# Graph attention block on one core: another order of work ahead of the first weight product

## The chip, the cores and the metric

The kernel runs on one core of one Trainium2 chip, as one program launch. The metric is the device time of that core in microseconds (us). TensorE, VectorE, ScalarE, GpSimd and SyncE (the queue SP, which only starts transfers here) each have their own instruction stream and meet at semaphores.

## The reference

With x of 384 rows by 1024 features, h = relu(layernorm(x)), and then a graph attention of 16 heads whose projections each consist of two matrices in a row:

```python
h = jnp.maximum(_layernorm(x, axis=-1), 0.0)
q = x @ wq.T + bq;   k = x @ wk.T + bk;   v = x @ wv.T + bv          # x is h here
q2 = (q @ wiq.T + biq)...; k2 = (k @ wik.T + bik)...; v2 = (v @ wiv.T + biv)...   # 16 heads of 64
mask = _build_mask(edge_index, edge_type, edge_type_weights, x.dtype)  # 384x384, from 6528 edges
scores = einsum('hnd,hmd->hnm', q2, k2) * scale + mask[None]
out = einsum('hnm,hmd->hnd', softmax(scores), v2)
return x + out @ wo.T + bo
```

(The lines are run together here.) Everything is float32. The part that the change touches is the layer norm of h and the first two of the eight column tiles of v = h @ wv.T + bv.

## The kernel before, in words

**Split numbers.** TensorE multiplies in a reduced form of float32 (fp32r). So each operand is kept as a high part (the value rounded by a copy, `..._hi`) and a low part (value minus high part, `..._lo`), and each product of two 128-wide blocks is three matmuls: high by high, low weight by high activation, high weight by low activation (`products`, L849, L850, L851). A weight slab is 128x1024 numbers; a stage of 1024 output columns has eight. A slab is fetched by SP into one of three places of `raw` (L305), ScalarE makes its high part (`split_hi`, L456), VectorE or GpSimd its low part (`split_lo`, L712 and L374), and TensorE then does one tile with it: 8 blocks k of the contraction times three matmuls of 384 columns. A place of `raw` comes free for the next transfer when the low part is made.

**The beginning.** The rows of x come as three tiles t of 128 rows (`x_sb`). For each, VectorE takes the statistics (L679, L683) and the variance plus epsilon (L685), GpSimd raises it to the power -1/2 (`rstd`, L367, after `memset`s and an `iota`), and for tiles 0 and 1 ScalarE makes h in one operation (L476). Tile 2 is the last and is done in another way, in halves of 512 columns: VectorE subtracts the mean and takes the maximum with 0 (L689, both halves while GpSimd works on the power), then ScalarE multiplies the first half by `rstd` in two pieces of 256 columns (L482, semaphore `h_ok`), and VectorE the second half (L693, `h_last_ok`). TensorE turns h in blocks of 128x128 (`turn_h`, L894) so that features lie on partitions: block k of all three tiles goes to one PSUM bank, `h_bank[k]`. When the block of tile 2 is there (`h_turned`), ScalarE copies the bank to `a_hi[k]` (L486, `h_hi`), and VectorE makes `a_lo[k]` from bank and high part (L725, `h_lo`). Blocks are turned as their scalings come: 0 to 6 of tiles 0 and 1 at once, with dummy matmuls (`warm`, L890, counts in `WARM`) between, block 7 of all tiles only inside the first tile.

**The first slab.** Its high part is made in halves: the first by ScalarE (L467, `half_hi`), the second by VectorE after the scaling (L695, `early_hi`). GpSimd makes both low parts (L384; `half_lo`, then `slab_lo`), and then, whole, that of slab 1 (L374).

**The first tile** (`first_tile`, L922, L923, L929) does for each k high by high, low weight, low activation. Its first matmul waits for `half_lo` and `h_hi`. The three late turns of tile 2 stand behind its second matmul. Tile 1 and all later ones are done by `tile` (L849 to L851), which waits for the whole low part of its slab. ScalarE's order between the copies to `a_hi` is written out: five of them, then the high part of slab 1, then three more, then the high part of slab 2.

Of the kernel before, what the change touches and what calls it, by code (L numbers as in the profile page):

```python
# [20 lines left out]
P = 128  # L21
N = 384
# [30 lines left out]
WARM = [18, 4, 3]  # L53
# [17 lines left out]
def gat_kernel(nc, slabs, x, edge_cols, edge_rows, edge_weights, biases, bo, out):  # L71
    with ExitStack() as ctx:
# [89 lines left out]
        h_bank = [bank[4], bank[7], bank[3], bank[5], bank[0], bank[1], bank[2], bank[4]]  # L162
# [31 lines left out]
        half_hi, half_lo, early_hi = sem("half_hi"), sem("half_lo"), sem("early_hi")  # L194
# [9 lines left out]
        y_ok, out_done, out_ok, stored = sem("y_ok"), sem("out_done"), sem("out_ok"), sem("stored")  # L204

# [137 lines left out]
        def _(pool):  # L343
# [107 lines left out]
        def _(act):  # L451
# [16 lines left out]

            for t in range(NT):
                act.dma_start(x_sb[:, t, HALF:F], x[t * P:(t + 1) * P, HALF:F]).then_inc(x_in[t][1], 16)  # L470
            for t in range(NT):
# [127 lines left out]
        def _(dve):  # L599
# [123 lines left out]
            for k in range(KT):  # L723
                dve.wait_ge(h_hi, k + 1)
                nc.vector.tensor_tensor(a_lo[:, k, :], h_bank[k][:, 0:N], a_hi[:, k, :].bitcast(F32),  # L725
                                        ALU.subtract).then_inc(h_lo, 1)
            edge_sign()
# [118 lines left out]
        def _(pe):  # L846
# [10 lines left out]
            def tile(t, a_h, a_l, ks=range(KT)):  # L857

                hi, lo = split_slab(slab_of(t))
# [5 lines left out]
                for k in ks:  # L865
                    c = slice(k * P, (k + 1) * P)
                    mm = products(psum[:, 0:N], (hi[:, c], lo[:, c]), (a_h[:, k, :], a_l[:, k, :]), k == 0,
# [24 lines left out]
            def turn_h(k, t):  # L892

                mm = nc.tensor.transpose(h_bank[k][:, t * P:(t + 1) * P], x_sb[:, t, k * P:(k + 1) * P], ident[:])  # L894
# [7 lines left out]
            for t in range(NT - 1):  # L902
                pe.wait_ge(h_ok, t + 1)
                for k in range(KT - 1):
                    turn_h(k, t)
                warm(WARM[t + 1])
            for b in range(2):
                pe.wait_ge(h_ok, NT + b)
                for k in range(2 * b, 2 * b + 2):
                    turn_h(k, NT - 1)  # L910

            def first_tile():

                hi, lo = split_place(0)
                psum = tile_place(0)[3]
                pe.wait_ge(half_lo, 1)
                for k in range(KT):
                    c = slice(k * P, (k + 1) * P)
# [208 lines left out]
```

## Time and profile before

| what | before |
|---|---|
| median of 3 runs | 295.54 us (295.51 to 296.37) |
| the profiled execution | 295.47 us |
| its span | 293.7 us |
| outside the span | 1.8 us |
| TensorE busy | 287.4 us (98%) |
| VectorE, ScalarE, GpSimd busy | 176.7, 153.5, 150.7 us |
| granted TensorE clock, mean | 0.998 |

The span runs from the first to the last instruction. A start in a timeline row is us from the span's start; a second number is how long the row's work took. Instructions of one engine are pipelined: the next may start shortly before the one ahead is shown as ended.

### The profile page before, as it was taken

To read this page: it belongs to the slowest core of one execution; us is meant where nothing else is said; L and a number is where in the kernel's file an instruction comes from. 1 tells how busy PE (TensorE), PEld (TensorE's weight loads), DVE (VectorE), ACT (ScalarE), POOL (GpSimd) and SP (SyncE) were. 2 spreads that over 40 slices of the span, in tenths; PEclk is the share of its full clock that TensorE was granted. 3 is DMA by queue.
4 is the path that set the end of the run, shared out by engine and by line. 5 is a ranking of instruction groups with operands and counts; after the bars stand their busy time and mean duration, and the time that the engine had idled before them with its cause. 6 is when DMAs were issued, how large, how long until landed. Compare 5 with 4: busy or idle time off the path is not lost.

```text
span 293.7 us, 4994 instructions
## 1 busy us (share of the span) xinstructions
PE 287.4 (98%) x1813; PEld 266.4 (91%) x1813; DVE 176.7 (60%) x475; ACT 153.5 (52%) x288; POOL 150.7 (51%) x153
## 2 busy tenths in 40 slices
PE   6899999999999999999999999999999999999996
PEld 3699998888899999999999999999999997888885
DVE  4999778786544534454467766665747475835241
ACT  2876443152523443244324685969687879874100
POOL 6552455543464455545300797758393939874000
PEclk9999999999999999999999999999999999999999
DMA  7978955749733443334654043140403132400032
GB/s 257 332 230 264 315 191 180 232 153 301 270 105 117 139 143 136 91 134 145 182 193 145 0 141 106 46 144 0 145 10 136 41 106 71 144 1 2 0 143 71
DMA packets 15818, 40.84 MB, mean 139 GB/s; under 512 B 3481, under 2 KB 4914, under 8 KB 15794
## 3 DMA queue, kind: packets, MB, share of 16 engines
q1 hardware_dynamic: 13346, 38.53, 39.2%
q0 software_dynamic: 2016, 1.21, 1.8%
q10 hardware_dynamic: 432, 0.79, 0.7%
q8 instruction: 14, 0.23, 0.3%
q14 instruction: 10, 0.08, 0.1%
HBM read 37.71 MB, written 2.81 MB: 138 GB/s over the span
## 4 chain that ended last, share of the span: by engine, by line
PE 95%; DMA 2%; ACT 1%; DVE 0%; SPq 0%; issue 0%
PE banks L849 27%; PE banks L850 26%; PE banks L851 26%; PE banks L966 5%; PE banks L1009 3%; PE banks L1010 3%; PE banks L981 3%; DMA x_sb<-in_x 2%; PE banks L994 1%; PE banks L894 1%; PE banks L922 1%; PE banks L929 0%; PE banks L923 0%; ACT x_sb L476 0%; SPq L289 0%; DVE stats L679 0%
## 5 line engine op out<-in xcount | busy, mean ns | idle before, releaser
L403 POOL DMA_INDIRECT cells<-value,cell x51 | 54.8, 1074 | 59.2 <-DMA cells<-value,cell 45.9
L456 ACT ACTIVATE w_hi<-raw 128x1024 fp32r<-128x1024 f32 x51 | 53.8, 1055 | 17.5 <-PE banks L851 17.3
L849 PE MATMUL banks<-a_hi,w_hi 128*128 128x384 f32 x184 | 61.5, 334 | 0.0
L850 PE MATMUL banks<-a_hi,w_lo 128*128 128x384 f32 x184 | 61.5, 334 | 0.0
L851 PE MATMUL banks<-a_lo,w_hi 128*128 128x384 f32 x184 | 61.5, 334 | 0.0
L712 DVE TENSOR_TENSOR w_lo<-raw,w_hi 128x1024 fp32r<-128x1024 f32 x36 | 44.0, 1223 | 12.6 <-ACT w_hi L456 12.5
L429 POOL TENSOR_SCALAR prob<-prob,row_inv 128x384 f32<-128x384 f32 x36 | 22.5, 640 | 43.6 <-DVE row_inv L779 43.6
L374 POOL TENSOR_TENSOR w_lo<-raw,w_hi 128x1024 fp32r<-128x1024 f32 x15 | 36.0, 2404 | 0.9 <-ACT w_hi L456 0.9
L849 PEld LDWEIGHTS banks<-a_hi,w_hi 128*128 128x128 f32 x184 | 34.5, 188 | 0.1
L850 PEld LDWEIGHTS banks<-a_hi,w_lo 128*128 128x128 f32 x184 | 34.5, 188 | 0.0
L851 PEld LDWEIGHTS banks<-a_lo,w_hi 128*128 128x128 f32 x184 | 34.5, 188 | 0.0
L783 DVE TENSOR_TENSOR pt_lo<-banks,pt_hi 128x384 fp32r<-128x384 f32 x48 | 23.8, 551 | 13.3 <-ACT pt_hi L548 13.1
L461 ACT ACTIVATE b_hi<-banks,bias 128x384 fp32r<-128x384 f32 x16 | 9.3, 581 | 35.0 <-PE banks L851 35.0
L534 ACT ACTIVATE prob<-prob,neg_max 128x384 f32<-128x384 f32 x36 | 21.8, 606 | 9.2 <-DVE neg_max L769 9.2
L548 ACT ACTIVATE pt_hi<-banks 128x384 fp32r<-128x384 f32 x48 | 20.1, 491 | 5.6 <-PE banks L1010 4.5
L849 PE MATMUL banks<-c_hi,w_hi 128*128 128x384 f32 x64 | 22.2, 346 | 0.0
L700 DVE SCALAR_TENSOR_TENSOR b_lo<-banks,bias,b_hi 128x384 fp32r<-128x384 f32 x16 | 9.9, 617 | 20.1 <-ACT b_hi L461 20.1
L849 PE MATMUL banks<-b_hi,w_hi 128*128 128x384 f32 x64 | 21.9, 343 | 0.0
L851 PE MATMUL banks<-b_lo,w_hi 128*128 128x384 f32 x64 | 21.4, 335 | 0.0
L851 PE MATMUL banks<-c_lo,w_hi 128*128 128x384 f32 x64 | 21.4, 334 | 0.0
L850 PE MATMUL banks<-c_hi,w_lo 128*128 128x384 f32 x64 | 21.4, 334 | 0.0
L850 PE MATMUL banks<-b_hi,w_lo 128*128 128x384 f32 x64 | 21.4, 334 | 0.0
(146 smaller groups left out, 610.1 us busy)
## 6 DMA issues: line engine op xcount, KB each, us to landing
raw<-in_slabs SPq DMA_DIRECT2D x56, 512.0 KB, 3.4
work<-key_rows SPq DMA_DIRECT2D x6, 256.0 KB, 5.3
prob<-key_rows SPq DMA_DIRECT2D x6, 256.0 KB, 3.8
x_sb<-in_x SPq DMA_DIRECT2D x3, 512.0 KB, 6.0
out_y<-x_sb SPq DMA_DIRECT2D x5, 256.0 KB, 2.1
cells<-prob SPq DMA_DIRECT2D x2, 576.0 KB, 7.9
cells<-value,cell POOLq DMA_INDIRECT x51, 2.6
x_sb<-in_x ACTq DMA_DIRECT2D x3, 256.0 KB, 4.3
```

The source lines that it names most:

```text
L374: nc.gpsimd.tensor_tensor(lo, raw[:, s % RAW, :], hi.bitcast(F32), ALU.subtract).then_inc(slab_lo, 1)
L403: nc.gpsimd.indirect_dma_start(out=cells[c][:, :], out_offset=bass.IndirectOffsetOnAxis(ap=cell[:, t:t + 1], axis=0), in_=value[:, t:t + 1 ...
L429: nc.gpsimd.tensor_scalar(probs[j % 2][x][:, n, :], probs[j % 2][x][:, n, :], row_inv[:, j % 2, c:c + 1], 1.0, ALU.mult, ALU.mult).then_in ...
L456: nc.scalar.activation(split_place(s)[0], raw[:, s % RAW, :], ACT.Copy).then_inc(slab_hi, 1)
L534: nc.scalar.activation(probs[j % 2][x][:, n, :], probs[j % 2][x][:, n, :], ACT.Exp, scale=-1.0, bias=neg_max[:, j % 2, c:c + 1], accum_out ...
L548: nc.scalar.activation(pt_as_placed(pt_hi, h, m), pt_place(h, m), ACT.Copy).then_inc(pt_hi_ok, 1)
L712: nc.vector.tensor_tensor(lo, raw[:, s % RAW, :], hi.bitcast(F32), ALU.subtract).then_inc(slab_lo_dve, 1)
L783: nc.vector.tensor_tensor(pt_as_placed(pt_lo, h, m), pt_place(h, m), pt_as_placed(pt_hi, h, m).bitcast(F32), ALU.subtract).then_inc(pt_lo_ ...
L849: nc.tensor.matmul(psum, w[0], a[0], start=first, stop=False)
L850: nc.tensor.matmul(psum, w[1], a[0], start=False, stop=False)
L851: return nc.tensor.matmul(psum, w[0], a[1], start=False, stop=last)
L966: mm = nc.tensor.matmul(score_bank(2 * n + x)[:, 0:N], q[own, turn, m], k[own, turn, :], start=(p == 0), stop=(p == 2))
```

## The change

It touches the beginning alone. In words:

1. VectorE does the second half of tile 2's subtract-and-maximum only when the power is there, instead of beside it, and then the multiply.
2. VectorE, not GpSimd, makes the low part of the first slab's first half, before `a_lo[0]`; the high part of the second half moves behind `a_lo[0]`. GpSimd makes only the second half's low part.
3. ScalarE's scaling of tile 2's first half is in pieces of 128, 128 and 256 columns; the third stands behind `a_hi[0]`.
4. TensorE turns all eight blocks of tiles 0 and 1 at once; block 7 goes to columns 384 to 511 of banks 0, 1 and 2. In the first tile, the first matmul waits only for `half_hi` and `h_hi`; the late turns (4 to 7, then 2 and 3, of tile 2) stand behind this one matmul, and the low weight and low activation matmuls of k = 0 and 1 come after.
5. ScalarE copies blocks 2 and 3 only when seven and eight blocks are turned, and makes the high part of slab 1 behind `a_hi[3]`, not behind `a_hi[4]`.
6. GpSimd makes the low part of slab 1 in two halves, and tile 1 starts on the first.
7. The dummy matmuls are 20, 5, 0 and 1 instead of 18, 4 and 3.

```diff
-WARM = [18, 4, 3]
+WARM = [20, 5, 0, 1]
...
-        h_bank = [bank[4], bank[7], bank[3], bank[5], bank[0], bank[1], bank[2], bank[4]]
+        h_bank = bank[0:6] + bank[7:8]
...
+        def h_turned_at(k, t):
+            return h_bank[k][:, t * P:(t + 1) * P] if k < KT - 1 else bank[t][:, N:N + P]
+        def h_all(k):
+            return h_bank[k][:, 0:N] if k < KT - 1 else banks[:, 0:NT, N:N + P]
...
                 hi, lo = split_place(s)
+                if s == 1:
+                    nc.gpsimd.tensor_tensor(lo[:, 0:HALF], raw[:, s, 0:HALF], hi[:, 0:HALF].bitcast(F32),
+                                            ALU.subtract).then_inc(second_lo, 1)
+                    nc.gpsimd.tensor_tensor(lo[:, HALF:F], raw[:, s, HALF:F], hi[:, HALF:F].bitcast(F32),
+                                            ALU.subtract).then_inc(slab_lo, 1)
+                    return
...
-            for b in range(2):
-                half = slice(b * HALF, (b + 1) * HALF)
-                pool.wait_ge((half_hi, early_hi)[b], 1)
-                nc.gpsimd.tensor_tensor(w_lo[:, 0, half], raw[:, 0, half], w_hi[:, 0, half].bitcast(F32),
-                                        ALU.subtract).then_inc((half_lo, slab_lo)[b], 1)
+            pool.wait_ge(early_hi, 1)
+            nc.gpsimd.tensor_tensor(w_lo[:, 0, HALF:F], raw[:, 0, HALF:F], w_hi[:, 0, HALF:F].bitcast(F32),
+                                    ALU.subtract).then_inc(slab_lo, 1)
...
-                    for part in (slice(0, HALF // 2), slice(HALF // 2, HALF)):
-                        nc.scalar.activation(x_sb[:, t, part], x_sb[:, t, part], ACT.Copy,
-                                             scale=rstd[:, t:t + 1]).then_inc(h_ok, 1)
+                    for part in (slice(0, P), slice(P, 2 * P)):
+                        scale_last(part)
             for k in range(KT):
-                act.wait_ge(h_turned, k + 1)
-                nc.scalar.activation(a_hi[:, k, :], h_bank[k][:, 0:N], ACT.Copy).then_inc(h_hi, 1)
-                if k == KT // 2:
+                if k == KT - 1:
+                    act.wait_ge(h_lo, NT)
+                act.wait_ge(h_turned, min(k + 1, KT) if k < 2 else min(k + 1 + KT // 2, KT))
+                nc.scalar.activation(as_turned(a_hi, k), h_all(k), ACT.Copy).then_inc(h_hi, 1)
+                if k == 0:
+                    scale_last(slice(2 * P, HALF))
+                if k == KT // 2 - 1:
                     split_hi(1)
...
                 h_last = x_sb[:, NT - 1, b * HALF:(b + 1) * HALF]
+                if b == 1:
+                    dve.wait_ge(rstd_ok, NT)
                 nc.vector.tensor_scalar(h_last, h_last, mean_var[:, NT - 1, 0:1], 0.0, ALU.subtract,
                                         ALU.max).then_inc(h_step, 1)
-            dve.wait_ge(rstd_ok, NT)
             dve.wait_ge(h_step, 2)
             nc.vector.tensor_scalar(h_last, h_last, rstd[:, NT - 1:NT], None, ALU.mult).then_inc(h_last_ok, 1)
-            dve.wait_ge(slab_in[0], 16)
-            nc.vector.tensor_copy(w_hi[:, 0, HALF:F], raw[:, 0, HALF:F]).then_inc(early_hi, 1)
+            dve.wait_ge(half_hi, 1)
+            nc.vector.tensor_tensor(w_lo[:, 0, 0:HALF], raw[:, 0, 0:HALF], w_hi[:, 0, 0:HALF].bitcast(F32),
+                                    ALU.subtract).then_inc(half_lo, 1)
...
+                if k == 0:
+                    dve.wait_ge(slab_in[0], 16)
+                    nc.vector.tensor_copy(w_hi[:, 0, HALF:F], raw[:, 0, HALF:F]).then_inc(early_hi, 1)
...
+                pe.wait_ge(half_hi, 1)
+                pe.wait_ge(h_hi, 1)
+                nc.tensor.matmul(psum[:, 0:N], hi[:, 0:P], a_hi[:, 0, :], start=True, stop=False)
+                turn_late()
+                pe.wait_ge(h_ok, NT + 2)
+                for k in range(2, KT // 2):
+                    turn_h(k, NT - 1)
+
                 pe.wait_ge(half_lo, 1)
-                for k in range(KT):
-...
+                first_product(0, lo, a_hi)
+                pe.wait_ge(h_hi, 2)
+                first_product(1, hi, a_hi)
+                first_product(1, lo, a_hi)
+                for k in range(2):
+                    pe.wait_ge(h_lo, k + 1)
+                    first_product(k, hi, a_lo)
+                for k in range(2, KT):
                     if k == KT // 2:
                         wait_lo(pe, 0)
                     pe.wait_ge(h_hi, k + 1)
...
```

TensorE's order at the start of the first tile, before (L890 dummy matmuls, L894 turns, L922, L923 and L929 the three matmuls of a block):

```order
L890 MATMUL banks<-iota,above 128x384 x3
L894 MATMUL banks<-ident,x_sb 128x128 [waits h_ok]
L894 MATMUL banks<-ident,x_sb 128x128
L894 MATMUL banks<-ident,x_sb 128x128 [waits h_ok]
L894 MATMUL banks<-ident,x_sb 128x128
L922 MATMUL banks<-a_hi,w_hi 128x384 [waits h_hi,half_lo]
L923 MATMUL banks<-a_hi,w_lo 128x384
L894 MATMUL banks<-ident,x_sb 128x128 [waits h_last_ok]
L894 MATMUL banks<-ident,x_sb 128x128 x2
L929 MATMUL banks<-a_lo,w_hi 128x384 [waits h_lo]
L894 MATMUL banks<-ident,x_sb 128x128 x3
L922 MATMUL banks<-a_hi,w_hi 128x384 [waits h_hi]
```

The same place of the changed kernel (L927 dummy matmul, L931 turns, L966 the first matmul, L962 the others):

```order
L931 MATMUL banks<-ident,x_sb 128x128 [waits h_ok] x2
L927 MATMUL banks<-iota,above 128x384
L966 MATMUL banks<-a_hi,w_hi 128x384 [waits h_hi,half_hi]
L931 MATMUL banks<-ident,x_sb 128x128 [waits h_last_ok]
L931 MATMUL banks<-ident,x_sb 128x128 x3
L931 MATMUL banks<-ident,x_sb 128x128 [waits h_ok]
L931 MATMUL banks<-ident,x_sb 128x128
L962 MATMUL banks<-a_hi,w_lo 128x384 [waits half_lo]
L962 MATMUL banks<-a_hi,w_hi 128x384 [waits h_hi]
L962 MATMUL banks<-a_hi,w_lo 128x384
L962 MATMUL banks<-a_lo,w_hi 128x384 [waits h_lo] x2
L962 MATMUL banks<-a_hi,w_hi 128x384 [waits h_hi]
```

Six turns, two of which were ahead of the first matmul, now stand in one block behind it, and the wait for the low part of the slab has moved from ahead of the first matmul to behind these turns.

ScalarE's order from the first slab's high part on, before (L467 that high part, L482 scalings, L486 copies to `a_hi`, L456 high parts of slabs 1 and 2):

```order
L467 ACTIVATE w_hi<-raw 128x512 [waits slab_in0]
L482 ACTIVATE x_sb<-x_sb,rstd 128x256 [waits rstd_ok,h_step]
L482 ACTIVATE x_sb<-x_sb,rstd 128x256
L486 ACTIVATE a_hi<-banks 128x384 [waits h_turned] x5
L456 ACTIVATE w_hi<-raw 128x1024 [waits slab_in1]
L486 ACTIVATE a_hi<-banks 128x384 [waits h_turned] x3
L456 ACTIVATE w_hi<-raw 128x1024 [waits slab_in2]
```

And of the changed kernel (L484, L488, L509 and L473 in their places):

```order
L484 ACTIVATE w_hi<-raw 128x512 [waits slab_in0]
L488 ACTIVATE x_sb<-x_sb,rstd 128x128 [waits rstd_ok,h_step]
L488 ACTIVATE x_sb<-x_sb,rstd 128x128
L509 ACTIVATE a_hi<-banks 128x384 [waits h_turned]
L488 ACTIVATE x_sb<-x_sb,rstd 128x256
L509 ACTIVATE a_hi<-banks 128x384 [waits h_turned] x3
L473 ACTIVATE w_hi<-raw 128x1024 [waits slab_in1]
L509 ACTIVATE a_hi<-banks 128x384 [waits h_turned] x3
L509 ACTIVATE a_hi<-banks 128x384 [waits h_turned,h_lo]
L473 ACTIVATE w_hi<-raw 128x1024 [waits slab_in2]
```

A third scaling stands between the first two copies, and the high part of slab 1 has moved up past the copy of block 4.

## Rows read from the trace of the kernel before

**Rows 1.** The page: span, TensorE's busy time, and the chain that ended last
```profile
span 293.7 us, 4994 instructions
PE 287.4 (98%) x1813; PEld 266.4 (91%) x1813; DVE 176.7 (60%) x475; ACT 153.5 (52%) x288; POOL 150.7 (51%) x153
...
PE 95%; DMA 2%; ACT 1%; DVE 0%; SPq 0%; issue 0%
```

**Rows 2.** Chain of waits, 8 to 17.5 us: start us, us, what
```profile
11.46 0.50 ACT a_hi L486
...
12.10 0.41 PE banks L922
```

**Rows 3.** Timeline, TensorE: start us, us, line, operation, tiles, shape, count
```profile
12.10 0.41 PE L922 MATMUL banks<-a_hi,w_hi 128*128 128x384 f32 x1 [0.22 <-ACT a_hi L486]
12.35 0.34 PE L923 MATMUL banks<-a_hi,w_lo 128*128 128x384 f32 x1
12.52 0.49 PE L894 MATMUL banks<-ident,x_sb 128*128 128x128 f32 x3
...
13.94 0.34 PE L922 MATMUL banks<-a_hi,w_hi 128*128 128x384 f32 x1
...
16.89 0.34 PE L929 MATMUL banks<-a_lo,w_hi 128*128 128x384 f32 x1
17.07 0.35 PE L849 MATMUL banks<-a_hi,w_hi 128*128 128x384 f32 x1
```

**Rows 4.** Timeline, ScalarE, 9 to 16 us
```profile
10.48 0.91 ACT L482 ACTIVATE x_sb<-x_sb,rstd 128x256 f32<-128x256 f32 x2 [0.16 <-POOL rstd L367]
...
11.46 2.02 ACT L486 ACTIVATE a_hi<-banks 128x384 fp32r<-128x384 f32 x5
...
13.33 1.10 ACT L456 ACTIVATE w_hi<-raw 128x1024 fp32r<-128x1024 f32 x1
...
14.28 1.30 ACT L486 ACTIVATE a_hi<-banks 128x384 fp32r<-128x384 f32 x3
```

**Rows 5.** Timeline, GpSimd, 5.5 to 17 us
```profile
5.78 0.57 POOL L367 TENSOR_TENSOR rstd<-var_eps,minus_half 128x1 f32<-128x1 f32 x1 [1.22 <-DVE var_eps L685]
...
9.63 0.75 POOL L367 TENSOR_TENSOR rstd<-var_eps,minus_half 128x1 f32<-128x1 f32 x1 [1.41 <-DVE var_eps L685]
10.39 1.28 POOL L384 TENSOR_TENSOR w_lo<-raw,w_hi 128x512 fp32r<-128x512 f32 x1
...
12.37 1.28 POOL L384 TENSOR_TENSOR w_lo<-raw,w_hi 128x512 fp32r<-128x512 f32 x1 [0.70 <-DVE w_hi L695]
...
14.50 2.41 POOL L374 TENSOR_TENSOR w_lo<-raw,w_hi 128x1024 fp32r<-128x1024 f32 x1 [0.85 <-ACT w_hi L456]
```

**Rows 6.** Timeline, VectorE, 9 to 19 us
```profile
9.47 0.87 DVE L689 TENSOR_SCALAR x_sb<-x_sb,mean_var 128x512 f32<-128x512 f32 x2
...
10.46 1.50 DVE L693 TENSOR_SCALAR x_sb<-x_sb,rstd 128x512 f32<-128x512 f32 x1
11.87 0.41 DVE L695 CAST w_hi<-raw 128x512 fp32r<-128x512 f32 x1
...
12.21 2.40 DVE L725 TENSOR_TENSOR a_lo<-banks,a_hi 128x384 fp32r<-128x384 f32 x5
...
17.20 1.21 DVE L712 TENSOR_TENSOR w_lo<-raw,w_hi 128x1024 fp32r<-128x1024 f32 x1
```

**Rows 7.** Groups by form, 9 to 17.3 us: count, busy us, mean ns of one
```profile
L725 DVE TENSOR_TENSOR a_lo<-banks,a_hi 128x384 fp32r<-128x384 f32 x8 | 3.9, 546 | 0.2 <-ACT a_hi L486 0.2
...
L482 ACT ACTIVATE x_sb<-x_sb,rstd 128x256 f32<-128x256 f32 x2 | 0.9, 501 | 0.2 <-POOL rstd L367 0.2
L689 DVE TENSOR_SCALAR x_sb<-x_sb,mean_var 128x512 f32<-128x512 f32 x2 | 0.9, 480 | 0.0
```

**Rows 8.** Groups by form, TensorE: dummy matmuls of 2.4 to 5.7, then of 7.4 to 9.5 us
```profile
L890 PE MATMUL banks<-iota,above 128*128 128x384 f16 x11 | 3.7, 520 | 2.5 <-POOL above L357 2.5
...
L890 PE MATMUL banks<-iota,above 128*128 128x384 f16 x4 | 0.8, 326 | 0.0
```

More of the change, by code:

```diff
@@ L193, in gat_kernel @@
         h_turned, h_hi, h_lo = sem("h_turned"), sem("h_hi"), sem("h_lo")
-        half_hi, half_lo, early_hi = sem("half_hi"), sem("half_lo"), sem("early_hi")
+        half_hi, half_lo, early_hi, second_lo = sem("half_hi"), sem("half_lo"), sem("early_hi"), sem("second_lo")
         slab_hi, slab_lo, slab_lo_dve, slab_used = sem("slab_hi"), sem("slab_lo"), sem("slab_lo_dve"), sem("slab_used")
@@ L467, in first_slab_hi, with scale_last @@
                 nc.scalar.activation(w_hi[:, 0, half], raw[:, 0, half], ACT.Copy).then_inc(half_hi, 1)
+            def scale_last(part):
+                nc.scalar.activation(x_sb[:, NT - 1, part], x_sb[:, NT - 1, part], ACT.Copy,
+                                     scale=rstd[:, NT - 1:NT]).then_inc(h_ok, 1)
             for t in range(NT):
@@ L724, in _ @@
                 dve.wait_ge(h_hi, k + 1)
-                nc.vector.tensor_tensor(a_lo[:, k, :], h_bank[k][:, 0:N], a_hi[:, k, :].bitcast(F32),
+                nc.vector.tensor_tensor(as_turned(a_lo, k), h_all(k), as_turned(a_hi, k).bitcast(F32),
                                         ALU.subtract).then_inc(h_lo, 1)
+                if k == 0:
+                    dve.wait_ge(slab_in[0], 16)
+                    nc.vector.tensor_copy(w_hi[:, 0, HALF:F], raw[:, 0, HALF:F]).then_inc(early_hi, 1)
             edge_sign()
@@ L857, in tile @@
             def tile(t, a_h, a_l, ks=range(KT)):
-                hi, lo = split_slab(slab_of(t))
+                if t == 1:
+                    hi, lo = split_place(t)
+                    pe.wait_ge(second_lo, 1)
+                else:
+                    hi, lo = split_slab(slab_of(t))
                 if t > 3 * KT + 6:
@@ L866, in tile @@
                     c = slice(k * P, (k + 1) * P)
+                    if t == 1 and k == KT // 2:
+                        wait_lo(pe, t)
                     mm = products(psum[:, 0:N], (hi[:, c], lo[:, c]), (a_h[:, k, :], a_l[:, k, :]), k == 0,
@@ L903, in _, with turn_late @@
                 pe.wait_ge(h_ok, t + 1)
-                for k in range(KT - 1):
+                for k in range(KT):
                     turn_h(k, t)
                 warm(WARM[t + 1])
-            for b in range(2):
-                pe.wait_ge(h_ok, NT + b)
-                for k in range(2 * b, 2 * b + 2):
+            for k in range(2):
+                pe.wait_ge(h_ok, NT + k)
+                turn_h(k, NT - 1)
+            warm(WARM[NT])
+            def turn_late():
+                pe.wait_ge(h_last_ok, 1)
+                for k in range(KT // 2, KT):
                     turn_h(k, NT - 1)
@@ L915, in first_tile, with first_product @@
                 psum = tile_place(0)[3]
-                pe.wait_ge(half_lo, 1)
-                for k in range(KT):
-                    c = slice(k * P, (k + 1) * P)
+                def first_product(k, w, a, stop=False):
+                    return nc.tensor.matmul(psum[:, 0:N], w[:, k * P:(k + 1) * P], a[:, k, :], start=False, stop=stop)
+                pe.wait_ge(half_hi, 1)
[4 more added lines that the diff above has]
+                for k in range(2, KT // 2):
+                    turn_h(k, NT - 1)
+                pe.wait_ge(half_lo, 1)
+                first_product(0, lo, a_hi)
+                pe.wait_ge(h_hi, 2)
+                first_product(1, hi, a_hi)
+                first_product(1, lo, a_hi)
+                for k in range(2):
+                    pe.wait_ge(h_lo, k + 1)
+                    first_product(k, hi, a_lo)
+                for k in range(2, KT):
                     if k == KT // 2:
@@ L921, in first_tile @@
                     pe.wait_ge(h_hi, k + 1)
-                    nc.tensor.matmul(psum[:, 0:N], hi[:, c], a_hi[:, k, :], start=(k == 0), stop=False)
-                    nc.tensor.matmul(psum[:, 0:N], lo[:, c], a_hi[:, k, :], start=False, stop=False)
-                    if k == 0:
-                        pe.wait_ge(h_last_ok, 1)
-                        for late in range(KT // 2, KT - 1):
-                            turn_h(late, NT - 1)
+                    first_product(k, hi, a_hi)
+                    first_product(k, lo, a_hi)
                     pe.wait_ge(h_lo, k + 1)
-                    mm = nc.tensor.matmul(psum[:, 0:N], hi[:, c], a_lo[:, k, :], start=False, stop=(k == KT - 1))
-                    if k == 0:
-                        for t in range(NT):
-                            turn_h(KT - 1, t)
+                    mm = first_product(k, hi, a_lo, stop=(k == KT - 1))
                 mm.then_inc(slab_used, 1)
```

4 lines of the change are left out of this document (3 added, 1 removed).

## The prediction

> **What bounds the kernel now.** First the page [rows 1]: TensorE is busy 98% of the span and carries 95% of the chain that ended last. So a change of the beginning counts by one thing alone: when TensorE goes over into its unbroken run of products. Then the chain [rows 2] and the timelines [rows 3 to 6]. The first useful matmul starts at 12.10, 0.14 after ScalarE ended `a_hi[0]` (11.46 + 0.50), not after the low part of the slab, which GpSimd had ready at 11.67 [rows 5]. From the next k on TensorE has no gap: from 13.94 to 16.89 it starts 18 matmuls, so one per 0.174 us, and tile 1 starts at 17.07 [rows 3]. That last instant is my yardstick: after it everything is the same program, and what tile 1 starts earlier or later goes into the time one to one.
>
> **The power, part 1 of the change.** The third power lasts 0.75 where VectorE works on x beside it, the first 0.57, where it doesn't [rows 5]. It ends at 10.38, just as the second VectorE piece does (9.47 + 0.87 = 10.34 [rows 6]). With that piece moved behind it I take 0.56: it ends at 10.19, 0.19 earlier. The bounds are 10.19 and, if nothing is won, 10.38.
>
> **The first turned block, part 3.** ScalarE starts its scaling 0.10 after the power (10.38, 10.48 [rows 4, 5]), so now at 10.29; its slab part ahead of it is done by then. A piece of 256 columns takes 0.50 [rows 7], and the next starts 0.41 after it (0.91 - 0.50 [rows 4]). A piece of 128 isn't in the trace: between half and all of 0.50; I take the middle, 0.38, and 0.29 to the next start. The first piece ends at 10.67, the second at 10.96. The turn follows 0.06 behind the first and takes 0.33 after a wait, which gives 11.06, and `a_hi[0]` starts at 11.10 instead of 11.46 and ends at 11.60. The first product starts 0.14 later, at **11.74, 0.36 earlier** than before. With the bounds (no gain on the power, 0.50 for the piece) it is 12.05, so this part gives 0.05 to 0.36.
>
> **Turns behind the first product, part 4.** The first matmul holds the next back by 0.25 (12.10 to 12.35 [rows 3]), and a turn costs 0.11 ((0.49 - 0.27)/2, [rows 3]). The late turns thus start at 11.99, the fifth (block 2) at 12.43, the sixth at 12.54; the fifth ends at 12.70. VectorE must have scaled its half: subtract from 10.24, 0.48 long [rows 7], multiply from 10.83, and with GpSimd idle it needs 0.48 and not the 1.50 that it has beside GpSimd's low part now [rows 6], so 11.31: in time. Two more turns of tiles 0 and 1 go ahead, in the time until the scaled piece comes: free. The dummy matmuls of part 7 end before anything they could hold.
>
> **The low parts, parts 1, 2 and 6.** On VectorE a low part of 512 columns lies between 0.55 (384 columns, [rows 7]) and 1.21 (1024, [rows 6]); I take 0.65. So `half_lo` at 11.88, ahead of the turns' end: free. Then `a_lo[0]` ends 12.35, the cast 12.68, `a_lo[1]` 13.15. GpSimd's second half follows 0.08 behind the cast and takes 1.28 [rows 5]: 14.04, before 13.65. TensorE wants it for k = 4, later than that. What SP waits to load into that place is 0.4 late and is used three tiles of 24 x 0.174 = 4.2 us on: free.
>
> **Where the gain goes.** ScalarE has to wait for seven turned blocks before `a_hi[2]` and so starts it at 12.74; before, it ran five copies without a gap from 11.46. Copies start 0.37 apart ((2.02 - 0.50)/4, [rows 4]), so the high part of slab 1 starts at 13.48, and `a_hi[4]`, now behind it, comes 0.95 later (13.33 to 14.28 [rows 4]): from 14.43 to 14.95. Before, `a_hi[4]` stood ahead of that high part and was ready at 13.48. TensorE, which after its last turn (12.54 + 0.11) does eleven matmuls of 0.174, would be at k = 4 at about 14.56, or 14.65 with the small waits for `a_lo[2]`. It starts there at 15.0: **a new gap of 0.35 to 0.45**. `a_lo[4]` starts on VectorE at 14.99, is ready at 15.54 [rows 7], and its matmul starts at 15.59, where two matmuls behind 15.0 and the 0.25 after a wait would be 15.42: another 0.15. From there nothing holds (`a_lo` comes every 0.47, three matmuls take 0.52): 0.25 later the next of the nine left starts, 15.84, the ninth at 17.23, and **tile 1 starts at about 17.40**. It needs the first half of slab 1's low part: high part ready 14.58, plus 0.08 and 1.28, 15.94; the second half at 17.2, wanted 2.1 us into the tile. Free, but also worth nothing: whole, as in [rows 5] with 2.41, it would have come at 17.1, too.
>
> **The sum.** TensorE's work between the first product and tile 1 is 24 x 0.174 + 6 x 0.11 = 4.84 in both. Before, it took 17.07 - 12.10 = 4.97, so 0.13 of waits. Now it takes 17.40 - 11.74 = 5.66, so 0.82: about 0.4 for `a_hi[4]`, 0.15 for `a_lo[4]`, the rest in small waits and the 0.08 lost behind each. That is 0.69 more waiting against 0.36 won: +0.33. On the profiled execution's own time, 295.47 (span 293.7 and 1.8 around it), this gives 295.80. That execution stands 0.07 under the median of 295.54, so the median would be 295.87. I take **295.8**.
>
> **A rule against the trace.** That GpSimd and VectorE hold each other up is in the rows: the multiply of 512 columns lasts 1.50 beside a GpSimd low part that ends at 11.67, the like operation 0.48 without one [rows 5, 6, 7]. The Trainium skill, page "SBUF — State Buffer", section on the two separate sides, says that the pair of ports that the two share is an exclusive lock for a whole instruction, and that the loser fully blocks. That agrees for the multiply. For the power it would mean a start only when VectorE lets go. Applied to this kernel as its own mechanism: the first VectorE piece still runs from 9.47 to about 9.95, the power would begin there and last 0.56 from then, to 10.51, 0.13 later than now instead of 0.19 earlier. Against this speaks that the power ended 0.04 after VectorE's second piece, too short for a whole power [rows 5, 6]; so most of it had run beside VectorE.
>
> **The rivals.**
>
> - *The gain stays.* `a_hi[4]` comes in time after all, because the high part of slab 1 holds ScalarE for less, or block 2 is turned earlier. Then TensorE runs on from 11.74: 24 x 0.174 + 6 x 0.11 + some 0.2 after waits put tile 1 at 16.8, 0.3 earlier: 295.2. For it: before, TensorE never waited in this stretch. Against it: the order of ScalarE is fixed, and 0.95 behind 13.48 is a plain sum. Chance 0.22.
> - *The power is not shorter.* It ends at 10.38 or, by the lock, at 10.51: 0.19 to 0.32 on every later instant of the path: 296.0 to 296.1. Chance 0.12. With this the change doesn't do what its first part says.
> - *Slower: the clock falls.* From 2.4 to 5.7 us eleven dummy matmuls run at 0.52 each, the lower level (1.2 GHz), after an idle start; those from 7.4 on, with the engine kept at work, at 0.33, the upper (2.4 GHz) [rows 8]. The changed kernel leaves TensorE idle at 11.3 to 11.7, 14.6 to 15.0 and 15.4, with no dummy matmuls there. If the clock fell in these gaps and a stretch as long as that first one, 3.3 us, ran at half speed, half of it would be lost: 1.65, 297.5. It decides at the first product that takes 0.52 or more. Against it: the gap ahead of the first product of before (0.22 idle, [rows 3]) cost no clock, and the new ones are little longer. The page "TensorE: Matmul & The Clock Gate" of the Trainium skill, Part 1, says that the low level is the default and activity lifts it, which leaves such a fall open. Chance 0.04.
>
> **How the numbers follow.** Forecast (new gap at k = 4, 295.6 to 296.1): 0.62. What one run in three showed before (296.37 beside 295.51 and 295.54) may shift a median by up to 0.8, whichever case holds; this widens the top. The range holds the forecast, the gain that stays and the unshortened power: **295.1 to 296.4**. A measurement of this kernel can tell about 0.3%, 0.9 us, from no change. For faster than that tile 1 would have to start at 16.2, which the sum of matmuls behind 11.74 (4.8 us) excludes; 0.02 for what I don't see. Slower: the clock, 0.04, and a high median, 0.03, so 0.07. Same: 0.91.
>
> **What would show it.** Right: the power near 0.56; `a_hi[0]` at 11.1; first product at 11.7; ScalarE idle or held about 0.4 before `a_hi[2]`; a gap on TensorE before the matmuls of k = 4, put down to `a_hi`; tile 1 at 17.3 to 17.5; all later tiles shifted by the same. Wrong: no gap at k = 4, tile 1 before 17.07, a power that ends after 10.4, or 0.33 us between any two matmul starts after 12 us.

## The result, and the profile after

The changed kernel takes **295.98 us** (median of 22 runs, 295.83 to 296.23), the kernel before, on the same chip, 295.48 (22 runs, 295.31 to 296.37). The ratio is 1.0017, with a 95% interval of 1.0012 to 1.0023: half a microsecond slower, inside the 0.3% that were called no change, and clear of zero. The prediction was 295.8. (In the later comparisons some executions, of the kernel before too, took 297.7 us and more; they widen the intervals below and move the ratios away from the quotients of the medians.)

| what | before | after |
|---|---|---|
| profiled execution | 295.47 us | 296.13 us |
| its span | 293.7 us | 294.4 us |
| third power, GpSimd | 0.75 us | 0.72 us |
| first product starts | 12.10 | 12.10 |
| tile 1 starts | 17.07 | 17.81 |

The two profiled executions don't start alike. The first tile of x arrived 0.29 us later in the second (VectorE's statistics start at 4.27 instead of 3.98), VectorE runs late by that, and its variance operation of the last tile (L685, now L710) starts at 9.59 instead of 9.40. Among all the profiles below that start lies between 9.31 and 9.59, whatever the kernel. So my measure from here on is the time **from the start of that operation to the start of tile 1**: 7.67 before (17.07 - 9.40), 8.22 after (17.81 - 9.59), 0.55 more.

GpSimd's timeline of the changed kernel, answering to [rows 5]:

```profile
9.82 0.72 POOL L380 TENSOR_TENSOR rstd<-var_eps,minus_half 128x1 f32<-128x1 f32 x1 [1.31 <-DVE var_eps L710]
...
14.99 1.28 POOL L388 TENSOR_TENSOR w_lo<-raw,w_hi 128x512 fp32r<-128x512 f32 x1 [0.63 <-ACT w_hi L473]
```

The first half of slab 1's low part is ready at 16.27, long before tile 1. VectorE's, answering to [rows 6]:

```profile
9.59 0.15 DVE L710 TENSOR_SCALAR var_eps<-mean_var 128x1 f32<-128x1 f32 x1
9.66 0.48 DVE L717 TENSOR_SCALAR x_sb<-x_sb,mean_var 128x512 f32<-128x512 f32 x1
10.57 0.48 DVE L717 TENSOR_SCALAR x_sb<-x_sb,mean_var 128x512 f32<-128x512 f32 x1 [0.44 <-POOL rstd L380]
11.10 0.49 DVE L720 TENSOR_SCALAR x_sb<-x_sb,rstd 128x512 f32<-128x512 f32 x1
11.50 0.68 DVE L722 TENSOR_TENSOR w_lo<-raw,w_hi 128x512 fp32r<-128x512 f32 x1
...
13.61 1.02 DVE L753 TENSOR_TENSOR a_lo<-banks,a_hi 128x384 fp32r<-128x384 f32 x2 [0.16 <-ACT a_hi L509]
15.32 1.95 DVE L753 TENSOR_TENSOR a_lo<-banks,a_hi 128x384 fp32r<-128x384 f32 x4 [0.69 <-ACT a_hi L509]
```

VectorE stood still for 0.44 while GpSimd worked, and yet the power lasts 0.72. The multiply is down from 1.50 to 0.49. Then VectorE waits 0.69 for ScalarE before `a_lo[4]`. ScalarE's timeline says why (answering to [rows 4]):

```profile
10.64 0.69 ACT L488 ACTIVATE x_sb<-x_sb,rstd 128x128 f32<-128x128 f32 x2
11.46 0.49 ACT L509 ACTIVATE a_hi<-banks 128x384 fp32r<-128x384 f32 x1
11.85 0.50 ACT L488 ACTIVATE x_sb<-x_sb,rstd 128x256 f32<-128x256 f32 x1
12.25 0.48 ACT L509 ACTIVATE a_hi<-banks 128x384 fp32r<-128x384 f32 x1
13.09 0.87 ACT L509 ACTIVATE a_hi<-banks 128x384 fp32r<-128x384 f32 x2 [0.36 <-PE banks L931]
13.85 1.06 ACT L473 ACTIVATE w_hi<-raw 128x1024 fp32r<-128x1024 f32 x1
14.80 1.64 ACT L509 ACTIVATE a_hi<-banks 128x384 fp32r<-128x384 f32 x4
```

It waits 0.36 for TensorE's turns before `a_hi[2]`, then makes two copies and the high part of slab 1, and only then, at 14.80, `a_hi[4]`. On TensorE (answering to [rows 3]; L962 are all matmuls of the first tile but the first):

```profile
12.10 0.41 PE L966 MATMUL banks<-a_hi,w_hi 128*128 128x384 f32 x1 [0.22 <-ACT a_hi L509]
12.35 0.82 PE L931 MATMUL banks<-ident,x_sb 128*128 128x128 f32 x6
...
14.85 0.33 PE L962 MATMUL banks<-a_lo,w_hi 128*128 128x384 f32 x1
15.43 0.41 PE L962 MATMUL banks<-a_hi,w_hi 128*128 128x384 f32 x1 [0.25 <-ACT a_hi L509]
15.68 0.34 PE L962 MATMUL banks<-a_hi,w_lo 128*128 128x384 f32 x1
15.93 0.44 PE L962 MATMUL banks<-a_lo,w_hi 128*128 128x384 f32 x1
...
17.81 0.33 PE L880 MATMUL banks<-a_hi,w_hi 128*128 128x384 f32 x1
```

The matmul after the one at 14.85 could start at 15.02 and starts at 15.43: the gap at k = 4 is 0.41. The idle figure in that row counts from the modelled end of the matmul ahead, so it reads 0.25. Last, the chain of waits of the changed kernel in this stretch (start us, us, what):

```profile
13.48 0.49 ACT a_hi L509
13.96 0.95 ACT w_hi L473
14.91 0.39 ACT a_hi L509
15.30 0.14 issue
15.43 2.53 PE banks L962 x12
```

The path that was TensorE's alone from 12.10 on now leads over ScalarE's high part of slab 1.

### The profile page after: what moved, and what is told of

It reads as the page before. It is cut to its first block, busy times and chain, and to the rows that moved or that the text cites. A ratio compares the mean times of both kernels' runs of the same rounds, so it can differ in the third digit from the quotient of the medians.

```text
span 294.4 us, 4998 instructions
## 1 busy us (share of the span) xinstructions
PE 287.9 (98%) x1814; PEld 266.3 (90%) x1814; DVE 176.0 (60%) x476; ACT 153.8 (52%) x289; POOL 150.3 (51%) x153
## 4 chain that ended last, share of the span: by engine, by line
PE 95%; ACT 1%; DMA 1%; DVE 1%; issue 0%; POOL 0%
PE banks L880 27%; PE banks L881 26%; PE banks L882 26%; PE banks L1021 5%; PE banks L1064 3%; PE banks L1065 3%; PE banks L1036 3%; PE banks L1049 1%; DMA x_sb<-in_x 1%; PE banks L931 1%; PE banks L962 1%; ACT a_hi L509 1%; DVE stats L704 0%; ACT x_sb L498 0%; ACT w_hi L473 0%
## 5 line engine op out<-in xcount | busy, mean ns | idle before, releaser
L420 POOL DMA_INDIRECT cells<-value,cell x51 | 56.3, 1103 | 58.5 <-DMA cells<-value,cell 46.5
L473 ACT ACTIVATE w_hi<-raw 128x1024 fp32r<-128x1024 f32 x51 | 53.7, 1053 | 17.4 <-PE banks L882 17.3
L393 POOL TENSOR_TENSOR w_lo<-raw,w_hi 128x1024 fp32r<-128x1024 f32 x14 | 33.6, 2408 | 0.0
```

Source lines behind the costliest of these rows:

```text
L420: nc.gpsimd.indirect_dma_start(out=cells[c][:, :], out_offset=bass.IndirectOffsetOnAxis(ap=cell[:, t:t + 1], axis=0), in_=value[:, t:t + 1 ...
L473: nc.scalar.activation(split_place(s)[0], raw[:, s % RAW, :], ACT.Copy).then_inc(slab_hi, 1)
```

## The experiments

Theory A: the loss is one of **ScalarE's order**; the first product's gain was small since the power wasn't shortened. Its rivals: that VectorE, with the slab's low part on it, is the limit; that the power or GpSimd is. One number for each run first. The runs came in three groups, each beside its own runs of the kernel before: e1 to e4 (median 295.46), e5 to e11 (295.54) and e12 to e15 (295.45).

| kernel | median us | ratio to before (95%) | variance to tile 1, us |
|---|---|---|---|
| before | 295.48 | | 7.67 |
| changed | 295.98 | 1.0017 (1.0012 to 1.0023) | 8.22 |
| e1_hi_late | 295.81 | 1.0002 (0.9977 to 1.0026) | 8.05 |
| e4_turns23_first | 295.70 | 1.0007 (0.9998 to 1.0016) | 7.87 |
| e2_beside | 296.05 | 1.0019 (1.0010 to 1.0028) | 8.29 |
| e3_both_behind | 296.26 | 1.0028 (1.0018 to 1.0037) | 8.49 |
| e5_pieces | 295.86 | 1.0021 (0.9996 to 1.0046) | 8.08 |
| e9_pool_lo_beside | 296.08 | 1.0020 (1.0002 to 1.0039) | 8.24 |
| e11_t23_hi5 | 295.36 | 1.0000 (0.9977 to 1.0023) | 7.60 |
| e10_t23_pieces_hi5 | 295.30 | 1.0007 (0.9977 to 1.0037) | 7.48 |
| e15_all_again | 295.25 | 0.9993 (0.9983 to 1.0002) | 7.61 |
| e12_all_chain_early | 295.21 | 0.9994 (0.9985 to 1.0003) | 7.47 |
| e13_whole_lo | 296.05 | 1.0013 (0.9996 to 1.0030) | 8.22 |
| e14_all_whole_lo | 296.04 | 1.0021 (1.0012 to 1.0030) | 8.16 |

The kernel before differs by 0.09 between its groups, so differences of 0.1 are at the limit of what the medians show, and I read them only where the last column agrees. That column can be split at the start of the first product. From the variance to there it is 2.70 before, 2.51 in the changed kernel, 2.78 in e3 and 2.38 in e5, e10, e12 and e14; from there to tile 1 it is 4.97 before, 5.70 or 5.71 in the changed kernel, e2, e3, e5, e9 and e13, 5.54 in e1, 5.36 in e4, and 5.08 to 5.10 in e10, e11, e12 and e15. All line numbers in rows are those of each run's own kernel.

**e1_hi_late: slab 1's high part behind block 4, as before.**

```diff
-                if k == KT // 2 - 1:
+                if k == KT // 2:
                     split_hi(1)
```

> The changed kernel with one thing undone: ScalarE makes the high part of slab 1 behind the copy of block 4, as before, not behind block 3. Theory A (what was lost hangs on ScalarE's order): a_hi[4] is ready at about 14.35, the gap ahead of the matmuls of k = 4 goes, but a_hi[5] now comes behind the high part, at 15.67 where TensorE wants it at 15.55, so about 0.3 of waiting comes back at k = 5; tile 1 at 17.6 instead of 17.81, time 0.15 to 0.2 us under the changed kernel, ratio to before about 1.001. Theory B (VectorE is the bound, since it got the slab's low part as work of its own): no change, tile 1 at 17.8, ratio 1.0017.

Measured: 295.81, 0.17 less; the last column falls by 0.17 as well. TensorE:

```profile
14.85 0.34 PE L962 MATMUL banks<-a_hi,w_hi 128*128 128x384 f32 x1
...
15.21 0.34 PE L962 MATMUL banks<-a_lo,w_hi 128*128 128x384 f32 x1
15.53 0.45 PE L962 MATMUL banks<-a_hi,w_hi 128*128 128x384 f32 x1
```

No gap at k = 4, and a smaller one one block on, as theory A said: the matmul at 15.53 could have started at 15.38, and the one with `a_lo[5]` loses another 0.13. Theory B expected no change: it falls.

**e4_turns23_first: the late turns in another order.** Block 7 of tile 2 must stay ahead of the copy of block 2, since both lie in bank 2.

```diff
-                turn_late()
+                pe.wait_ge(h_last_ok, 1)
+                turn_h(KT - 1, NT - 1)
                 pe.wait_ge(h_ok, NT + 2)
                 for k in range(2, KT // 2):
                     turn_h(k, NT - 1)
+                turn_late()
...
-                act.wait_ge(h_turned, min(k + 1, KT) if k < 2 else min(k + 1 + KT // 2, KT))
+                act.wait_ge(h_turned, k + 1 if k < 2 else min(k + 2, KT))
```

(`turn_late` itself turns only blocks 4 to 6 here, and no longer waits for `h_last_ok`.)

> The changed kernel with the turns behind the first product in another order: block 7 of tile 2, then blocks 2 and 3, then 4 to 6; ScalarE copies block 2 when four blocks are turned, not seven. Theory A: a_hi[2] starts at about 12.77 instead of 13.09, everything behind it on ScalarE 0.32 earlier, a_hi[4] ready at 14.97, no gap at k = 4, still 0.2 of waiting for a_lo[4]; tile 1 at 17.45, time 0.35 us under the changed kernel, ratio to before 1.0005. Theory B (VectorE bound): its chain of a_lo starts as before, so at most 0.1 is won.

Measured: 295.70, 0.28 less; last column 0.35 less. ScalarE:

```profile
12.25 1.39 ACT L509 ACTIVATE a_hi<-banks 128x384 fp32r<-128x384 f32 x3
13.53 1.06 ACT L473 ACTIVATE w_hi<-raw 128x1024 fp32r<-128x1024 f32 x1
14.48 1.64 ACT L509 ACTIVATE a_hi<-banks 128x384 fp32r<-128x384 f32 x4
```

`a_hi[4]` starts 0.32 earlier, at 14.48. Up to 14.07 on TensorE and up to `a_lo[1]` on VectorE everything starts within 0.01 of the changed kernel. The time fell, so theory A holds, but not its "no gap at k = 4":

```profile
14.77 0.34 PE L961 MATMUL banks<-a_lo,w_hi 128*128 128x384 f32 x1
15.11 0.41 PE L961 MATMUL banks<-a_hi,w_hi 128*128 128x384 f32 x1
```

The second could have started at 14.94, so 0.17 of the gap of 0.41 is left. `a_hi[4]` is ready at 14.97 as expected; I had left out the 0.14 that TensorE starts behind it. Both halves of the order, turns and high part, carry the loss.

**e2_beside and e3_both_behind: what holds the power up.** e2 puts VectorE's second piece beside the power again, e3 puts both behind it.

```diff
-                if b == 1:
+                if b == 0:
                     dve.wait_ge(rstd_ok, NT)
```

(e3; e2 has the wait behind the loop, as before.)

> The changed kernel with VectorE's second subtract-and-maximum beside the power again. Theory A (the power is held up by the first piece alone, which both kernels run beside it): the power stays at 0.72 to 0.75, time as the changed kernel within 0.1 us, ratio 1.0017. Theory B (the second piece lengthens it, as the prediction had it): the power gets longer by up to 0.2 and the time rises by as much, ratio 1.0023.

> The changed kernel with both subtract-and-maximum pieces behind the power, so that VectorE does nothing beside it. Theory A (the first piece holds the power up): the power lasts 0.55 to 0.58, 0.16 shorter; ScalarE's first scaling then waits for the first piece and starts at about 11.05 instead of 10.64, so the first product and tile 1 come about 0.4 later; ratio 1.003. Theory B (the third power is long for another reason, such as the transfers): it stays at 0.72 and the time rises by 0.55.

Measured: e2 296.05, 0.07 more, and e3 296.26, 0.28 more. The power in e2, then in e3:

```profile
9.65 0.75 POOL L380 TENSOR_TENSOR rstd<-var_eps,minus_half 128x1 f32<-128x1 f32 x1 [1.31 <-DVE var_eps L710]
```

```profile
9.67 0.55 POOL L380 TENSOR_TENSOR rstd<-var_eps,minus_half 128x1 f32<-128x1 f32 x1 [1.31 <-DVE var_eps L710]
```

With nothing beside it 0.55; with one piece 0.72 (in the changed kernel, e1, e4, e11 and e13 alike), with two 0.75 (before, e2 and e9). So the second piece, which the change moved away, was worth 0.03, and the **first**, which it left, holds the power up by 0.17. The time of e2 alone doesn't tell its theories apart: 0.07 is no more than the spread of the executions, and in its profile 0.04 of the 0.07 are from turns of tiles 0 and 1 that came late (ScalarE waits 0.16 for them before `a_hi[0]`). Theory A's price of 0.4 for e3 was too high. From the variance on, the first scaling starts 0.28 later than in the changed kernel (10.77 - 9.44 against 10.64 - 9.59): the engines followed each other 0.03 and 0.04 behind, where I had taken 0.07 and 0.10.

**e5_pieces: a shorter first piece.**

```diff
-            for b in range(2):
-                h_last = x_sb[:, NT - 1, b * HALF:(b + 1) * HALF]
+            for b, cols_h in enumerate((slice(0, 2 * P), slice(2 * P, HALF), slice(HALF, F))):
+                h_last = x_sb[:, NT - 1, cols_h]
```

(ScalarE waits for the second piece before its third scaling, VectorE for the third before its multiply.)

> The changed kernel with the subtract-and-maximum of the first 512 columns in two pieces of 256: one before the power, one behind it. Theory A (the power finishes 0.41 to 0.44 after the VectorE piece that runs when it starts has ended): the shorter piece lasts 0.34 instead of 0.48, the power ends 0.13 earlier (0.58 to 0.60 long), and the first product with it; the gap at k = 4 is of ScalarE's order and moves along, so the time falls by 0.1 to 0.13 against the changed kernel, ratio to before 1.0013. Theory B (the power has a length of its own in the third place): it stays at 0.72 and the time doesn't fall.

```profile
9.69 0.59 POOL L380 TENSOR_TENSOR rstd<-var_eps,minus_half 128x1 f32<-128x1 f32 x1 [1.31 <-DVE var_eps L711]
```

Measured: power 0.59, 0.13 less, last column 0.14 less, all of it ahead of the first product. The median is 0.12 less, and 0.18 less if each is taken against its own runs of the kernel before. The power's end follows the end of the piece it meets: 9.53 + 0.35 = 9.88 here, and 0.40 later 10.28; in the changed kernel 10.14 and 10.54. The rule fits all profiles with one piece beside the power (0.40 to 0.42 behind the piece); with two it is 0.43 to 0.44 behind the first.

**e9_pool_lo_beside: part 1 of the change and the low part of part 2 undone together.**

```diff
+            pool.wait_ge(half_hi, 1)
+            nc.gpsimd.tensor_tensor(w_lo[:, 0, 0:HALF], raw[:, 0, 0:HALF], w_hi[:, 0, 0:HALF].bitcast(F32),
+                                    ALU.subtract).then_inc(half_lo, 1)
             pool.wait_ge(early_hi, 1)
```

(The same operation goes from VectorE, and the wait on the power goes behind VectorE's loop. The high part of the slab's second half stays behind `a_lo[0]`, so part 2 isn't undone whole.)

> The changed kernel with its first two parts undone: the second subtract-and-maximum is beside the power again, and GpSimd makes the low part of the slab's first half, from the power's end on. Theory A (neither part is on the path, since the late turns stand behind the first product and the path goes over ScalarE): VectorE's multiply is held up to about 1.5 us again and ends at 12.1, but TensorE wants it only at 12.35; a_lo[0] starts at 12.1 as it does now; time as the changed kernel within 0.1, ratio 1.0017. Theory B (the parts are needed): the late turns wait for the multiply, and the time rises by 0.2 or more.

```profile
9.46 0.87 DVE L718 TENSOR_SCALAR x_sb<-x_sb,mean_var 128x512 f32<-128x512 f32 x2
10.45 1.49 DVE L722 TENSOR_SCALAR x_sb<-x_sb,rstd 128x512 f32<-128x512 f32 x1
11.86 0.54 DVE L752 TENSOR_TENSOR a_lo<-banks,a_hi 128x384 fp32r<-128x384 f32 x1
```

Measured: 296.08, the last column 8.24 against 8.22. The multiply takes 1.49 again, and nobody notices. So in this order of work neither part does anything for the time beyond the 0.03 of the power; in the repaired order of e11 it wasn't tried. VectorE gains a microsecond on the multiply and spends it on the wait and the low part, and the late turns behind the first product don't need either.

**e11_t23_hi5 and e10_t23_pieces_hi5: the repairs together.** Turns as in e4, slab 1's high part behind block 5 (`if k == KT // 2 + 1`); e10 has the pieces of e5 besides.

> The turns in the other order (block 7, 2, 3, then 4 to 6), and the high part of slab 1 behind the copy of block 5. Theory A (all that was lost is ScalarE's order against TensorE's need): every a_hi from 2 to 5 comes 0.37 apart from 12.77 on, a_hi[6] at 15.7 and a_hi[7] at 16.1 ahead of TensorE's need at 16.1 and 16.6, no gap over 0.1; the low half of slab 1 is ready at 16.7; tile 1 at about 16.95 where the changed kernel has 17.81 and the kernel before, with the same start of tile 2's work, 17.26: 0.85 us under the changed kernel, 0.3 under the kernel before, ratio 0.999. Theory B (VectorE's added work is a second limit right behind): tile 1 at 17.2 at best, ratio 1.000.

> The kernel of the run before with the first 512 columns in two pieces of 256 as well. Theory A: another 0.1 to 0.13 less, ratio to before 0.9985. Theory B (VectorE is the limit by then, and a third piece adds work to it): the same time as without the pieces, or up to 0.1 more.

Measured: e11 295.36, 0.62 under the changed kernel and 0.18 under the kernel before beside it; by the last column 0.62 and 0.07. e10 295.30. The ratios, 1.0000 and 1.0007, don't show a gain over the kernel before. TensorE in e11:

```profile
15.88 0.34 PE L961 MATMUL banks<-a_hi,w_lo 128*128 128x384 f32 x1
16.10 0.45 PE L961 MATMUL banks<-a_lo,w_hi 128*128 128x384 f32 x1
16.39 0.34 PE L961 MATMUL banks<-a_hi,w_hi 128*128 128x384 f32 x1
...
16.91 0.33 PE L880 MATMUL banks<-a_hi,w_hi 128*128 128x384 f32 x1
```

The gap at k = 4 is gone and TensorE runs on, but for `a_lo[6]` (16.10 instead of 16.06, and 0.12 more behind it) and the turns. 0.85 were expected. Theory A has the mechanism right and its size too high by 0.23: I had left out the 0.08 that TensorE loses behind the turns, and this wait with its 0.12. The pieces give 0.06 by the median and 0.12 by the last column, with 0.1 to 0.13 expected. That column is 7.61 in e15, the same kernel as e10: in that profile the dummy matmuls still last 0.50 on the mean from 7.4 to 8.3 us, where those of e10 last 0.33, so the turns of tiles 0 and 1 come late, ScalarE waits 0.28 for them before `a_hi[0]`, and the first product comes 0.15 later. VectorE, which theory B made the limit, holds TensorE at this one place only.

With these orders long executions are more frequent: 4 of the 12 of e10 (297.72 to 300.34) and 2 of the 12 of e11 (298.37 and 300.09), against 3 of 59 of the other kernels measured beside them. By the mean e11 (295.99) is 0.4 above the kernel before beside it (295.59), not below.

**e12_all_chain_early and e15_all_again.** e15 is e10 once more. e12 also lets ScalarE and VectorE do tile 2's parts before slab 5's, and VectorE the first edge unit before slab 5's low part.

```diff
...
-                if s < 2:
+                if s < 3:
                     tile_lo_part(s)
+                if s == UNITS_FROM:
+                    edge_unit(0)
                 if lo_by_vector(s + AHEAD):
...
```

> The kernel with turns in the other order, the two pieces of 256 and slab 1's high part behind block 5, and besides: in the step of tile 2, ScalarE and VectorE do tile 2's parts before slab 5's, and VectorE the first edge unit before slab 5's low part. Theory C (the runs of the kernel without this that are 2 to 5 us longer come from the mask: GpSimd's row of scattered transfers began 2.4 us later there, because the first cells came behind slab 5, and TensorE then waits for VectorE, held by the mask): the first cells come at 28.5 instead of 30.6, as before, and none of some 12 runs is over 297; median 295.2 to 295.3, ratio 0.999. Theory D (the long runs have nothing to do with the mask's start): as many of them as without.

> The same kernel as the run with turns in the other order, two pieces and slab 1's high part behind block 5, once more, beside the kernel with the mask's start moved up. Theory C: median 295.3 again, and some of its runs 2 to 5 us longer. Theory D (those runs came by chance that day): none.

Measured: 295.21 and 295.25, both 0.2 under the 295.45 of the kernel before beside them; their intervals just reach past 1, so that they beat it by the median is likely and not shown. The first cells come at 28.1 in e12, 29.2 in e15 and 28.2 in the kernel before. But e12 had executions of 299.85 and 300.75 among its 12, e15 one of 299.62 among 11, and the kernel before itself had 298.19 and 301.25 among 35. **Theory C is not borne out**: an earlier start of the mask did not remove the long runs. Whether they are due to the mask's end by its varying length, or to something else, stays open. What the record does show is that they go with the repaired orders: 9 of 47 executions of e10, e11, e12 and e15, but 6 of 223 of the kernel before and of the eight other kernels that keep slab 1's high part ahead of `a_hi[5]`, and none of 11 in e14, where tile 1 starts later. By the mean of all executions e12 (296.13) is above the kernel before beside it (295.70) and e15 (295.65) level with it.

**e13_whole_lo and e14_all_whole_lo: part 6 undone,** in the changed kernel and in the repaired one (GpSimd's low part of slab 1 whole, tile 1 waits for `slab_lo`).

> The changed kernel with slab 1's low part whole again, in one operation of 2.41 us. Theory A: it is ready at 17.4 where tile 1 starts at 17.8, so nothing changes, ratio 1.0017; the halves bring nothing in this kernel. Theory B (GpSimd's low part is a limit of tile 1's start already): 0.2 or more on the time.

> The kernel with the three repairs (turns, pieces, slab 1's high part behind block 5) with slab 1's low part whole. Theory A: ready at 15.1 + 2.41 = 17.5, so tile 1 starts at 17.65 instead of 16.87 and 0.75 us are lost, ratio 1.001 to 1.0015; there the halves are worth 0.75. Theory B (they are worth nothing here either): ratio 0.999.

Measured: e13 296.05, last column unchanged at 8.22. e14 296.04, that is 0.79 over e15. (The last column, 8.16, ends at the start of tile 1 and so misses the 0.11 that TensorE loses behind that wait.) Its GpSimd and TensorE:

```profile
15.18 2.40 POOL L387 TENSOR_TENSOR w_lo<-raw,w_hi 128x1024 fp32r<-128x1024 f32 x1 [0.80 <-ACT w_hi L467]
```

```profile
16.76 0.33 PE L950 MATMUL banks<-a_lo,w_hi 128*128 128x384 f32 x1
17.63 0.44 PE L875 MATMUL banks<-a_hi,w_hi 128*128 128x384 f32 x1 [0.54 <-POOL w_lo L387]
```

The halves of slab 1 are worth nothing in the changed kernel, and 0.8 once TensorE would otherwise be there at 16.93.

## Why the prediction was right, and where it wasn't

The range, the direction and the class held: 0.33 more were forecast, 0.50 were measured. The mechanism, a new gap at k = 4, is the one that was forecast; the number 295.98, though, is that of a rival, the power that is not shorter (296.0 to 296.1, chance 0.12), which came true beside it. By its own steps:

- **The power: wrong.** The step "with that piece moved behind it I take 0.56" failed. It had put the 0.75 down to the second piece, because the two ended together. e3 shows 0.55 only when the first piece goes, too. The bound "if nothing is won" held: 0.03 won of 0.19. This is that rival in its mild form. The sign "a power that ends after 10.4" also appeared (10.54; 10.35 without the 0.19 by which VectorE started later in this profile). The lock of the Trainium skill's page "SBUF — State Buffer", applied in the prediction as a whole power after the first piece, gave 0.13 more than before; the trace gives 0.40 after the piece's end instead of the 0.56. An estimate from these two: some 0.15 of the power had run before it was held.
- **The first turned block: right.** Pieces of 128 columns last 0.40 and 0.38 (0.38 taken), their starts 0.31 apart (0.29 taken). From the variance to the first product there are 2.51 (12.10 - 9.59) where there were 2.70: 0.19 won. Without the power's 0.16 the predicted 0.36 would have been 0.20.
- **Turns and low parts: right.** Six turns from 12.35 on, 0.11 apart, the multiply 0.49, the low part of 512 columns on VectorE 0.68 (0.65 taken), `half_lo` at 12.18 ahead of the turns' end. Hidden, and e9 shows that they would have been hidden either way.
- **The new gap: right.** 0.35 to 0.45 was predicted, 0.41 is there, for the reason given; e1 takes it away, e4 more than half of it, and both together with one block more (e11) leave none. Some luck is in the sizes: the prediction let TensorE start 0.05 behind `a_hi[4]` where it is 0.14, and took the wait for `a_lo[4]` at 0.15 where it is 0.08 (15.93, not 15.85), which nearly cancel. The distance of ScalarE's copies, (2.02 - 0.50)/4, is 0.38 and not 0.37.
- **The sum.** From the first product to tile 1 it is 17.81 - 12.10 = 5.71, predicted 5.66. So the term that was mis-sized is the power: 0.36 - 0.19 = 0.17 too much gain, 0.16 of it the power's, against the 0.17 by which the median missed (0.22 by the last column, with the 0.05 of the stretch behind).
- **The clock: right not to hold.** No two matmuls after 12 us lie 0.33 apart without a wait. That the granted clock reads 1.00 over the whole span is the weaker sign: it reads 1.00 from 2.4 to 5.7 us of the kernel before too, where the dummy matmuls last 0.52.
- **The gain that stays** did not happen here. e11 comes near it: 0.18 under the kernel before by the median, 0.07 by the start of tile 1, with 0.3 in the rival, and not shown against the long executions. The change had the parts of a faster kernel (turns behind the product, halves of slab 1), with an order on ScalarE that gave it all back.

## What to carry to other kernels

When the first of a chain of operations is moved up, count when the fourth and fifth come: here one matmul started 0.19 earlier, and the copy that TensorE needs 3 us later, `a_hi[4]`, was ready 1.6 later (5.70 after the variance instead of 4.08), since it had to wait for turns and a big operation had been put ahead of it. An operation that is off the path may be cut from 1.5 to 0.5 without any effect; ask first who waits for it. And a part worth nothing in one order (halving the slab) can be worth 0.8 in the next, so parts of a change are to be judged in the combination in which they are kept.

## What the runs showed of the hardware

- **GpSimd's power and VectorE.** It takes 0.55 with nothing beside it (e3). If VectorE's subtract-and-maximum (`TENSOR_SCALAR`, 128x512 or 128x256 float32) runs when it starts, it ends 0.40 to 0.44 after that operation, whichever kernel; a next such operation beside it (before, e2 and e9) accounts for the upper 0.03 of this. Not every VectorE operation does it: the statistics operation, on as many numbers, runs beside the first power of the kernel before, which still takes 0.57 [rows 5]:

```profile
5.61 0.68 DVE L679 BATCH_NORM_STATS2 stats<-x_sb 128x6 f32<-128x512 f32 x1
```

  The other way round, a VectorE multiply that meets a GpSimd subtract waits for it: 1.49 in e9 against 0.49 in the changed kernel. This agrees with the exclusive lock of the Trainium skill, "SBUF — State Buffer", section on the two separate sides, except that the power isn't held in full: it ends 0.40 after the piece and not 0.55.
- **TensorE after a wait.** The first matmul of 384 columns after a wait holds the next off by 0.25 to 0.29 instead of 0.174: 12.10 to 12.35, 15.43 to 15.68 and 15.93 to 16.21 in the changed kernel, 15.53 to 15.82 in e1. A gap of 0.41 thus costs 0.5.
- **The clock and a long wait.** In the one profile of e10, of a 299.23 us execution, the mask came late and TensorE waited 2.2 for `k_lo`. Windows of that profile (start and end, length, busy us of the engines, clock, transfers):

```profile
158.00:160.00 2.00, 0.04 (x1) 0.00 (x0) 2.00 (x3) 0.58 (x1) 0.00 (x0) 1.00 0.00 0
160.00:162.00 2.00, 1.75 (x14) 1.75 (x16) 2.00 (x4) 0.00 (x0) 0.00 (x0) 0.70 0.65 170
162.00:164.00 2.00, 2.00 (x11) 1.56 (x8) 2.00 (x9) 1.64 (x5) 0.00 (x0) 0.50 0.82 250
```

and the two waits of 150 to 165 us that lead to the gap:

```profile
DVE prob L746 <- DMA prob<-cells: 4.8, 1, 4.8
...
PE banks L1023 <- DVE k_lo L729: 2.2, 1, 2.2
```

  TensorE had been busy until 158, was idle until 160.2, and the granted clock then stood at 0.50, the lower level, in the slice from 162 to 164. No matmul behind the gaps of 0.4 at the beginning was slower. Of the 15 long executions on record the ten of 299.2 us and more have a mean granted clock of 0.989 to 0.994, the five of 297.7 to 298.4 one of 0.999 or 1.000: so a lower clock goes with the longer ones only. The mask comes out of 51 scattered transfers on GpSimd, the last of which was issued between 139.8 and 143.7 in the profiles (139.9 before, 143.7 in this one). In the profile of the kernel before, `k_lo`, which VectorE makes behind the mask, was ready at 155.8 and wanted at 158.1: a margin of 2.3. Why the transfers ended so late here, no run settles; the first of them was issued 2.4 later than before (31.57 against 29.16), the last 3.8 later.
